# Second cross attention of a two-layer decoder: score banks and the place of the query projections

## The reference, cut to what matters

```python
def _L1_xattn_ref(key, query, mask, w_q, w_k, w_v, w_o):
    q = jnp.einsum('blj,njd->bnld', query, w_q)
    k = jnp.einsum('blj,njd->bnld', key, w_k)
    v = jnp.einsum('blj,njd->bnld', key, w_v)
    score = jnp.einsum('bnid,bnkd->bnik', q, k) / sqrt_d
    m = mask[:, None]
    score = score * m + NEG * (1.0 - m)
    attn = jax.nn.softmax(score, axis=-1)
    out = jnp.einsum('bnij,bnjk->bnik', attn, v)
    return jnp.einsum('bnlj,njk->blk', out, w_o)
...
x = x + _L1_xattn_ref(ctx_1024, _layernorm(x, axis=-1), mask_BxSxS2_fk1, ...)
```

## Time and profile before

| what | value |
|---|---|
| time, median of 3 runs | 1763.72 us |
| the profiled execution's own time | 1767.52 us |
| its span, first to last instruction | 1765.8 us |
| busy in the span: PE, DVE, ACT, POOL | 74%, 81%, 62%, 65% |
| the changed stage, from its first projection to its last addition | 1385.0 to 1692.5 us |
| granted TensorE clock, mean of the span | 0.883 |
| DMA share of the 16 engines in the stage | at most 0.20 in a stretch of 40 us |

### The profile page before, as it was taken

How to read it: one execution, slowest core, us unless ns; L and a number is a source line. 1 busy time by engine, 2 the same in 40 slices (tenths; PEclk the granted TensorE clock), 3 DMA queues, 4 the chain that set the end, 5 groups by cost and what they waited for, 6 DMA issues and landing times. The chain is left out here.

```text
span 1765.8 us, 23296 instructions
## 1 busy us (share of the span) xinstructions
PE 1315.4 (74%) x6904; PEld 648.2 (37%) x6907; DVE 1426.4 (81%) x2430; ACT 1101.4 (62%) x2435; POOL 1140.0 (65%) x742
## 2 busy tenths in 40 slices
PE   6777898986757656767567666667746799899979
PEld 4554565553322212222122222212201465566543
DVE  4654898978259999999999999999996477777845
ACT  4444887876566566676566666566644577777740
POOL 2101565651079999999999999999994144444410
PEclk9999999998878888798888888888867799999989
DMA  3000000000054453353443443543332311111000
GB/s 102 1 1 2 1 2 1 1 20 7 6 223 164 190 191 133 132 207 138 191 186 145 145 186 137 198 186 145 121 136 80 111 49 49 48 72 72 1 1 24
DMA packets 70215, 168.03 MB, mean 95 GB/s; under 512 B 20420, under 2 KB 40152, under 8 KB 56664
## 3 DMA queue, kind: packets, MB, share of 16 engines
q1 hardware_dynamic: 68680, 166.17, 25.6%
q10 hardware_dynamic: 1168, 0.53, 0.1%
q0 software_dynamic: 256, 0.01, 0.0%
HBM read 131.04 MB, written 35.65 MB: 94 GB/s over the span
## 5 line engine op out<-in xcount | busy, mean ns | idle before, releaser
L1633 POOL TENSOR_TENSOR ma_hs<-ma_dtuR,ma_Bt 128x1024 f32<-128x1024 f32 x256 | 596.6, 2358 | 7.0 <-DMA ma_dtuR<-ma_dtu_d 6.7
L1816 ACT ACTIVATE ps<-ma_dtR,ma_A 128x512 f32<-128x512 f32 x512 | 332.7, 682 | 297.2 <-DVE ma_hs L1961 254.8
L845 POOL TENSOR_TENSOR x_pr<-x_pr,x_rec 128x512 f32<-128x512 f32 x256 | 267.4, 1045 | 291.6 <-DVE x_rec L1085 291.6
L1955 DVE TENSOR_TENSOR_SCAN ps<-ps,ma_hs 128x1024 f32<-128x1024 f32 x176 | 401.5, 2281 | 0.2
L1710 PE MATMUL ps<-ma_hs,ma_fold 128*32 128x512 f32 x1024 | 174.7, 816 | 206.1 <-POOL ma_hs L1641 177.4
L1051 ACT ACTIVATE x_pr<-x_sm,x_mx 128x256 f32<-128x256 f32 x512 | 255.2, 500 | 68.9 <-DVE x_mx L1076 65.9
L1961 DVE TENSOR_TENSOR ma_hs<-ps,ma_Ct 128x1024 f32<-128x1024 f32 x176 | 215.4, 1224 | 6.1
L1955 DVE TENSOR_TENSOR_SCAN ma_hs<-ps,ma_hs 128x1024 f32<-128x1024 f32 x80 | 182.5, 2281 | 18.3 <-ACT ps L1816 15.4
L1641 POOL TENSOR_TENSOR ma_hs<-ma_hs,ma_Ct 128x1024 f32<-128x1024 f32 x80 | 188.2, 2353 | 12.3 <-DVE ma_hs L1955 12.1
L1677 PE MATMUL ps<-ma_hn,ma_w_tap 128*128 128x512 f32 (+3 forms) x256 | 142.0, 707 | 52.4 <-ACT ma_hn L1840 52.4
L907 PE MATMUL ps<-ident,x_pr 128*128 128x128 f32 x1024 | 163.2, 286 | 5.4 <-DVE x_pT L985 4.4
(11 more groups left out here) (304 smaller groups left out, 2168.6 us busy)
## 6 DMA issues: line engine op xcount, KB each, us to landing
ma_dtuR<-ma_dtu_d SPq DMA_DIRECT2D x32, 1024.0 KB, 6.7
ma_dtR<-ma_dt_d SPq DMA_DIRECT2D x32, 1024.0 KB, 8.7
ma_Bt<-ma_bc_d SPq DMA_DIRECT2D x16, 1024.0 KB, 5.0
ma_Ct<-ma_bc_d SPq DMA_DIRECT2D x16, 1024.0 KB, 7.4
ma_dtu_d<-ma_dtu SPq DMA_DIRECT2D x32, 256.0 KB, 2.0
ma_dt_d<-ma_dt SPq DMA_DIRECT2D x32, 256.0 KB, 2.3
keys_d<-ma_kv SPq DMA_DIRECT2D x32, 256.0 KB, 4.4
values_d<-ma_kv SPq DMA_DIRECT2D x32, 256.0 KB, 2.5
```

Source lines behind the costliest of these rows:

```text
L845: pool.tensor_tensor(pr[:, r, :, :], pr[:, r, :, :], rec[:, r, :].unsqueeze(2).broadcast_to([P, 2, L]), ALU.mult).then_inc(pr_done, 1)
L1633: pool.tensor_tensor(hs[:, k % SLOTS, :, :], dtuR[:, unit(f, h), q, :].unsqueeze(1).broadcast_to([P, 2, CH]), rows(Bt, k), ALU.mult).then_ ...
L1816: e = act.activation(c.ps[:, 2 * (k % 2) + a, :], dtR[:, unit(f, h), q, :], ACT.Exp, scale=A[:, (f // QUARTERS) % 2, h, q, no:no + 1])
L1955: dve.tensor_tensor_scan(out, pair(k), slot(k), 0.0, ALU.mult, ALU.add).then_inc(scan_done, 1)
```

## The change

For the second cross attention alone: the scores rotate through three banks (0, 1, 6) in place of two; all projection units use bank 7; the units of the next batch are made at items 9, 11, 13 and 15, one each; the first scores of each four heads wait for the one unit that makes their queries; and batch 0 makes only unit 0 ahead of its scores, and units 1, 2, 3 at items 1, 3 and 5. The pair of item n now waits until head n-2 has been read (`s_free` counts n-1), except that the first pair of an even batch, whose banks are those of the pair before it, waits for head 15 of that batch. The first cross attention keeps its banks, items and waits.

```diff
-    SCORE_BANKS = ((0, 1), (5, 7)) if small else ((0, 1),)
+    SCORE_BANKS = ((0, 1), (5, 7)) if small else ((0, 1), (6, 0), (1, 6))
...
-            return range(min(NP, a * 3 // 2), min(NP, (a + 1) * 3 // 2)) if a >= 0 else range(0)
+            if a < 0:
+                return range(0)
+            return range(a // 2, a // 2 + 1) if a % 2 else range(0)
...
-        def score_bank(n):
+        def score_bank(p, n):
 
-            return SCORE_BANKS[(n // 2) % len(SCORE_BANKS)][n % 2]
+            pair = n // 2 if small else n // 2 + p * NH // 2
+            return SCORE_BANKS[pair % len(SCORE_BANKS)][n % 2]
+
+        def first_units(n):
+
+            return range(n // 2 + 1, n // 2 + 2) if not small and n in (1, 3, 5) else range(0)
 
         def projection_bank(n):
 
-            return 6 if small else 6 + n % 2
+            return 6 if small else 7
...
-                    if small and n >= 1:
+                    if n >= 1:
                         pe.wait_ge(evac, b * NP + n)
-                    elif n >= 2:
-                        pe.wait_ge(evac, b * NP + n - 1)
                     elif not first:
                         pe.wait_ge(evac, b * NP)
-                    if 6 + n == WO and not first and not second:
+                    if n == 0 and not first and not second:
                         pe.wait_ge(x_done, b - 1)
...
-                    if n == 0:
+                    if small and n == 0:
                         pe.wait_ge(evac, b * NP + NQK)
-                        if not small:
-                            pe.wait_ge(k_in[p], b * 8 + 16 - 8 * p)
+                    if not small and n % 4 == 0:
+                        pe.wait_ge(evac, b * NP + n // 4 + 1)
+                    if not small and n == 0:
+                        pe.wait_ge(k_in[p], b * 8 + 16 - 8 * p)
...
-                        pe.wait_ge(s_free, b * NH + n)
+                        pe.wait_ge(s_free, b * NH + (n - 1 if n + p else 0))
...
-                for n in range(NP):
+                for n in range(NP if small else 1):
                     project(0, n, True, False)
...
                         if n % 2 == 0:
                             score_pair(b, p, n, first)
+                        if first:
+                            for a in first_units(n):
+                                project(0, a, True, False)
...
-                for n in range(NP):
+                for n in range(NP if small else 1):
                     evacuate(0, 0, n, True, False)
...
                     for n in range(NH):
+                        if first:
+                            for a in first_units(n):
+                                evacuate(0, 0, a, True, False)
```

More of the change, by code:

```diff
@@ L896, in score_pair @@
                             keys = km[row, p, n // 2, :] if small else k[row, p, n // 2, :]
-                            mm = pe.matmul(c.ps[:, score_bank(n + r), t * L:(t + 1) * L], queries, keys, start=True, stop=True)
+                            mm = pe.matmul(c.ps[:, score_bank(p, n + r), t * L:(t + 1) * L], queries, keys, start=True, stop=True)
                             if t == 1:
@@ L1067, in maximum @@
                     dve.wait_ge(scores, b * NH + n + 1)
-                    bank = c.ps[:, score_bank(n), :].rearrange("p (t k) -> p t k", t=2)
+                    bank = c.ps[:, score_bank(p, n), :].rearrange("p (t k) -> p t k", t=2)
                     if n >= 2 or not first:
```

## The result

The changed kernel took 1751.13 us (median of four runs, 1747.43 to 1755.21) against 1763.76 of the kernel before in the same series: ratio 0.9925, 95% interval 0.9909 to 0.9942. A second series on the same code gave 1748.79 (1748.07 to 1749.44) against 1764.17, ratio 0.991 (0.9894 to 0.9926). It is faster, by 13 to 15 us, where 19.5 were forecast; the forecast time was 1744.2.

A forecast was written before the change was run, and what follows sets the result against it. PE and DVE were taken to bound the stage in turn. Gains of 4.0 + 1.6 + 2.5 + 11.4 = 19.5 us bring the median from 1763.7 to 1744.2, range 1737 to 1756.

The forecast's parts named there:

- The bound: Steady batch: PE's work of 33.2 us plus its waits makes a period of 34.6 in place of 36.48.
- The wait at `finish`: Item 9: unit 0 uses the output projection's bank, so PE waits 0.6 us for `finish`.
- The waits at weigh: Items 4 and 6: PE's weigh waits 0.6 and 0.2 us for ACT's copies of turned heads.
- six distances: Steady part up to head 8 of batch 7: six gains of 1.9 us, 11.4 in all.
- DVE's wait at head 10: Steady batch: 0.3 us of DVE's 1.64 us wait for the scores of head 10 stays.
- Start: Stage's beginning: with only one unit ahead, head 0 reaches DVE 4.0 us earlier, range 3.6 to 4.5.
- Head 0 to 8: Batch 0: moved units fill part of PE's idle time, a gain of 1.6 us, between 0 and 2.6.
- Batch 0 to 1: Head 8 of batch 0 to that of batch 1: gain of 2.5 us, between 2.1 and 2.9.
- The third bank: Output projection: of one head's lead, 1.8 us, only 0.7 is left there.
- Behind it no units exist and nothing changes: Behind head 8 of batch 7: no further gain or loss was forecast.
- Rival (1): Steady batches: POOL and DVE collide more, even items lengthen, three lost ties of 1.5 us; gain 11, time 1753; 12%.
- Rival (4): Steady batches: small waits lower PE's clock for two pairs in each of seven batches, +38 us, time 1782; 6%.

The follow-up runs named there:

- e4: Changed kernel with DVE's addition of the output projection moved ahead of head 8's mask product: 1746.97 us, ratio 0.9896 to the kernel before.
- e10: Kernel before with only DVE's addition of the output projection moved ahead of head 8's mask product: 1763.65 us, ratio 0.9989.
- e1: Changed kernel run again, nothing edited: 1748.79 us, ratio 0.9910 to the kernel before.
- e2: Changed kernel with scores in banks 0 and 1 only and the wait for head n-1: 1755.29 us, ratio 0.9947 to the kernel before.
- e3: Changed kernel with all four units of batch 0 ahead of its scores, in the one bank 7: 1755.77 us, ratio 0.9950.
- e6: Changed kernel with five extra products, results unused, in the expert part: 1748.49 us, ratio 0.9912 to the kernel before.
- e5: Kernel before with five extra products, results unused, in the expert part: 1764.23 us, ratio 0.9998.
- e7: Changed kernel with the next batch's units back at items 8, 9, 9 and 10, all in bank 7: 1784.35 us, ratio 1.0120.
- e8: Changed kernel with the addition ahead of head 8's mask product and five extra products in the expert part: 1741.59 us, ratio 0.9878.
- e12: Same code as e8, run again: 1742.20 us, ratio 0.9869 to the kernel before.
- e11: Same code as e4, run again: 1745.15 us, ratio 0.9890 to the kernel before.
- e9: e4 with unit 0 of the next batch moved from item 9 to item 5: 1746.78 us, ratio 0.9900 to the kernel before.

## Why the prediction was right, and where it was off

The mechanism of the stage was right: which engine waits for which, at which items, and which waits go. Two sizes were off, and one thing was not in it, the clock outside the steady part. The stage gained 16.2 and 17.1 us where 19.5 were forecast. The first median, 1751.1, is inside the stated range of 1737 to 1756 but 1.1 above the 1739 to 1750 of the forecast's own bounds; the second, 1748.8, is inside both. It is partly luck that the start came out within 0.3 us: 0.4 too few at head 0 and 0.7 too many behind it.

- **The bound.** That PE's work plus its waits makes the period: measured 33.2 + waits = 35.0 against 34.6. As a sum it holds in any kernel. That PE is what bounds the batch from item 8 on is shown by e4, where removing one wait took its whole length off the batch, while the same edit did nothing in a batch of the kernel before (e10). In the other half DVE bounds, as forecast: it does not wait there, and PE waits for copies that hang on it.
- **The wait at `finish`.** Forecast 0.6, measured 0.81, from the end of weigh at 1508.27 to 1509.08 (0.74 by the row): `finish` starts 1.66 behind the mask product of head 8 as forecast, but PE starts 0.25 behind its end and not 0.07.
- **The waits at weigh.** Forecast 0.6 and 0.2, measured 0.53 (1531.75 less 1530.63 + 0.59) and 0.5, both on ACT's copies as forecast. Head 4 reached DVE at 1531.91 and its item took 1.84 (the next row of DVE starts at 1533.75), as an odd one does, where I had 1.66; the weigh of item 6 started 3.59 behind it, where I had 3.4. Together the three waits are 1.84 for 1.4: that is the 0.4 a batch, 2.2 us in the six distances (9.2 for 11.4). DVE's wait at head 10 was 0.67 where the walk left 0.3: unit 0 started later, and the item of head 9 took 1.65 where I had 1.83.
- **Start.** Head 0: 3.6 for 4.0, since the scores ran at the lower clock (2.08), the lower end I had named. Head 0 to 8: 2.3 for 1.6 (1.9 in e1). Batch 0 to 1: 2.5 for 2.5.
- **The third bank.** Forecast: only 0.7 us of the 1.8 of one more head's lead is left at the output projection, because weigh waits for ACT. Measured: 0.7 by e2.
- **What was not in it: the clock outside the stage.** "Behind it no units exist and nothing changes" is the step that failed in the first profile. 1.3 us were lost at the end of the stage and 4.9 in the expert part. In e1 both were absent (26.2 and 73.4). The loss in the last batch is no matter of the code either. PE idles 1.51 us there in both profiles, but only in the first did the clock fall behind it (0.57 from 1663 to 1667 us); the first profile and e1:

```profile
1663.00 1.97 PE L941 MATMUL ps<-x_pT,x_v 128*64 128x256 f32 x8 [1.51 <-ACT x_pT L997]
...
1662.63 1.08 PE L941 MATMUL ps<-x_pT,x_v 128*64 128x256 f32 x8 [1.51 <-ACT x_pT L997]
```

  Of the 7.2 us between the forecast 1748.0 of the profiled execution and its 1755.2, these are 6.2, the steady batches and the start 2.0, and 1.1 came back ahead of the stage. The sum also took 3.8 us off, since the profiled execution before was that much above its median. This need not carry over: e1's profiled execution is at its median, with the shorter rest.
- **Rival (1), the mask's offset and POOL.** In batches 2 to 5 the two operations start within 0.01 us of each other. In the changed kernel's two profiles, in e2, e3 and e6, and in the kernel before (and e5), DVE lost the tie in batch 5 and only there; in batches 2 to 4 it won, and POOL's operation took 1.32 us in place of 1.04:

```profile
1558.72 1.04 POOL L852 TENSOR_TENSOR x_pr<-x_pr,x_rec 128x512 f32<-128x512 f32 x1 [0.79 <-DVE x_rec L1098]
1558.72 1.32 DVE L1143 TENSOR_SCALAR x_neg<-x_m 128x512 f32 x1
```

  That batch was 1.5 us longer before and 0.9 after. The 0.9 is the tie, at a clock of 1.00, in e2 with two banks too. The 0.6 more before go with the lower clock: PE waited 1.86 us for the bank, and its next turn and weigh took 1.10 and 1.98 us in place of 0.66 and 1.08. So rival (1) priced a lost tie at 1.5 for the change, where it is 0.9. It is no draw in each batch but the same batch each time; the rival's three more lost ties did not come. Even items did not lengthen where they follow a wait or a copy; head 4, which now follows neither, did.
- **Rival (4), the clock falls in the steady part.** It stayed at 1.00 in all six steady batches, although PE now rotates through three banks with waits of 0.5 to 0.8. The swing of the clock that the Trainium skill warns of with such a rotation (TensorE: Matmul & The Clock Gate, "A second HAM failure mode: psum-queue depth-cycling") does not show in these batches. The rival's mechanism is real in this stage all the same, with longer waits: in e7, where PE waits 2.3 to 2.5 us once a batch, the clock falls in every batch, for 1.5 us. In the changed kernel the clock did cost time, but in the last batch and behind the stage.

What stays open: the runs of one kernel differ by up to 8 to 10 us, and in the profiles the first projection of the stage starts anywhere between 1378.4 and 1385.8, behind code that no edit touched. So part of the spread is made ahead of the stage, and whether the whole kernel gained 13 or 15 us cannot be said; that the stage gained 16 to 17 can, since its length repeats within 0.5 us in codes with the same stage, apart from the last batch of the first profile. Why the clock comes back earlier or later behind the stage stays open too.

## What to carry to other kernels

When two engines bound a loop in turn, add up one engine's work for a whole period and then list the waits that would be left on it. A deeper buffer helps only up to the next wait in its order, here 0.7 of 1.8 us. An operation that releases an in-order engine should stand in the other engine's idle time, not behind its next item. Here moving such an operation was worth its whole wait once the engine it releases was the bound, and nothing before that. A wait that hangs on the other engine is not won by filling it: the unit moved into one brought 0.2 us. A new wait can cost more than its length: in e7 one of 2.5 us lowered the clock for another 1.5. Where a part runs at a changing clock, its length can differ by several us between two executions of the same code, so read the gain from the stage, not from one total.

## What the runs showed of the hardware that was not expected

- Between two profiles of the same code the expert part took 73.4 and 78.2 us, with identical work: TensorE stayed at the lower clock for three experts instead of one, though it was busy almost without a gap from 1697 us on. Up to 1714 the granted clock is 0.50, with 16.93 of 17.00 us busy, and it rose only then; over the 20 us of this row it is 0.57:

```profile
1697.00:1717.00 20.00, 19.93 (x33) 5.93 (x34) 9.02 (x10) 0.00 (x0) 0.00 (x0) 0.57 0.00 0
```

- Extra products that kept the clock up ahead of that part moved the stretch at the lower level behind them: the rest is 74.3 to 74.4 us in all four profiles that have them, with either kernel, and 73.3 to 78.2 in the ten without.
- The same idle time of 1.51 us in the last batch was followed by the lower clock in the first profile of the changed kernel and not in e1, with the same code.
- The tie of DVE and POOL in batch 5 fell the same way in both profiles of each code that has two: lost in the changed kernel (first and e1) and in e8 and e12, won in e4 and e11. In e7, e9 and e10 it was won. With two profiles of each code this looks decided by the program and not by chance, and even by edits far from it, for e8 differs from e4 in the expert part alone; what in the program decides it is not shown.
